# Decoder block: the negated row maxima go into the transposed queries by a copy and two DMAs instead of two broadcasts

## The reference

```python
x = layernorm(x + attn(x))        # kernelised attention, 16 heads of 16, 64 random features
x = layernorm(x + xattn(ctx, x))  # softmax attention, queries from x, keys and values from ctx
x = layernorm(x + ffn(x))         # gated, activations to 8 bits, weights ternary
```

```python
kh, qh, vh = ctx_h @ Wk.T, x_h @ Wq.T, ctx_h @ Wv.T
attn = softmax(qh @ kh.T / sqrt(16))
out_h = attn @ vh
```

## Time and profile before

| | |
|---|---|
| time, median of 3 runs | 572.56 us (571.44 to 573.2) |
| profiled execution, span | 572.7 us |
| PE busy | 498.8 us, 87% |
| DVE busy | 473.8 us, 83% |
| ACT busy | 468.6 us, 82% |
| POOL busy | 387.8 us, 68% |
| mean granted clock of PE | 0.959 |

### The profile page before, as it was taken

How to read it: one execution, slowest core, us unless ns; L and a number is a source line. 1 busy time by engine, 2 the same in 40 slices (tenths; PEclk the granted TensorE clock), 3 DMA queues, 4 the chain that set the end, 5 groups by cost and what they waited for, 6 DMA issues and landing times.

```text
span 572.7 us, 17406 instructions
## 1 busy us (share of the span) xinstructions
PE 498.8 (87%) x5990; PEld 346.3 (60%) x5990; DVE 473.8 (83%) x1380; ACT 468.6 (82%) x843; POOL 387.8 (68%) x769
## 2 busy tenths in 40 slices
PE   3057999999999999999999999999999998977751
PEld 2034777666667666677776777776766666744310
DVE  0783566888989998999999999999999998998671
ACT  0225678999999998999999999999999999987631
POOL 7032665678776777777777777787788876665432
PEclk9995999999999999999999999999999999997775
DMA  5604765656676765656565656665555677353221
GB/s 137 220 0 76 139 121 110 105 119 113 132 129 131 130 118 111 130 118 130 112 127 116 129 114 126 121 125 116 124 121 120 127 122 120 84 113 65 36 48 37
DMA packets 191625, 64.01 MB, mean 112 GB/s; under 512 B 171360, under 2 KB 191328, under 8 KB 191584
## 3 DMA queue, kind: packets, MB, share of 16 engines
q1 hardware_dynamic: 189056, 60.32, 53.5%
q10 hardware_dynamic: 2528, 3.15, 1.7%
HBM read 17.31 MB, written 4.19 MB: 38 GB/s over the span
## 4 chain that ended last, share of the span: by engine, by line
ACT 25%; POOL 21%; PE 20%; issue 11%; DVE 9%; DMA 8%; SPq 4%; ACTq 1%; POOLq 1%; DVEq 0%
DMA hqT<-hq 6%; ACT tT L610 5%; PE bank L1081 4%; POOL pkA L410 4%; POOL hq L465 4%; POOL hq L470 3%; POOL rs L424 3%; ACT pT L616 2%; PE bank L1148 2%; ACT pT L617 2%; SPq L303 2%; ACT x L549 2%; POOL y L414 2%; ACT pkA L505 2%; PE bank L1294 2%
## 5 line engine op out<-in xcount | busy, mean ns | idle before, releaser
L1081 PE MATMUL bank<-wq_hi,xT 128*128 128x512 f16 (+1 forms) x256 | 72.0, 337 | 0.3
L610 ACT ACTIVATE tT<-bank 16x1024 f16<-16x1024 f16 x64 | 65.0, 1016 | 1.2
L460 POOL TENSOR_TENSOR xq<-xm,nmagic 128x256 bf16<-128x256 f32 x32 | 19.6, 614 | 66.4 <-DVE xm L908 66.4
L1148 PEld LDWEIGHTS bank<-kvm,phq 128*128 128x128 f32 x512 | 62.2, 192 | 2.5
L1148 PE MATMUL bank<-kvm,phq 128*128 128x34 f32 x512 | 59.8, 272 | 0.0
L410 POOL TENSOR_TENSOR pkA<-qk,pkA 128x512 f16<-128x512 f32 x32 | 37.5, 1173 | 32.9 <-ACT pkA L505 32.9
L424 POOL TENSOR_TENSOR rs<-ve,mhalf 128x1 f32<-128x1 f32 x96 | 52.8, 550 | 0.0
L1294 PE MATMUL bank<-downT,hqT 128*128 128x256 bf16 x256 | 34.6, 280 | 16.5 <-DMA hqT<-hq 16.4
L862 DVE TENSOR_REDUCE negm<-bank 128x4 f16<-128x512 f32 x64 | 43.8, 684 | 5.5 <-PE bank L1197 5.1
L1241 PE MATMUL bank<-pT,ctxv 128*32 128x128 f32 x1024 | 41.6, 281 | 6.8 <-ACT pT L617 6.7
L912 DVE SCALAR_TENSOR_TENSOR g<-th,bank 128x512 f32<-128x512 f32 x64 | 43.3, 676 | 4.0 <-ACT th L640 3.8
(11 more groups left out here) (180 smaller groups left out, 1637.3 us busy)
## 6 DMA issues: line engine op xcount, KB each, us to landing
xs<-in_x_dram SPq DMA_DIRECT2D x32, 128.0 KB, 2.7
xr<-in_x_dram SPq DMA_DIRECT2D x32, 128.0 KB, 2.5
cs<-in_ctx_dram SPq DMA_DIRECT2D x32, 128.0 KB, 2.6
out_dram<-ot SPq DMA_DIRECT2D x32, 128.0 KB, 2.1
ffn_ld<-in_L_ffn_w_gate_dram ACTq DMA_DIRECT2D x1, 1024.0 KB, 5.8
ffn_ld<-in_L_ffn_w_up_dram ACTq DMA_DIRECT2D x1, 1024.0 KB, 8.7
ffn_ld<-in_L_ffn_w_down_dram ACTq DMA_DIRECT2D x1, 1024.0 KB, 10.6
pkAT<-pkA SPq DMA_TRANSPOSE x64, 3.3
```

The lines of the kernel that those rows point to most:

```text
L610: last = sc.activation(tT[p + 32:p + 48, :, :], at_mT.bitcast(F16)[p + 32:p + 48, :].unsqueeze(1).to_broadcast([DK, PAIRS, P]), ACT.Copy)
L1081: last = T.matmul(o, xT[:, 2 * part + c, :], w[:, c, cols], start=(n == 0), stop=(n == 5))
L1148: last = T.matmul(at_num[:, 2 * DV * k:2 * DV * (k + 1)], phq[:, par, k, :], kvm[:, k, :, :].rearrange("p h d -> p (h d)"), start=False, s ...
```

## The change

One copy of 128x128 takes the transposed maxima from PSUM to a new tile nmT, and SP moves 8 partitions of it into one partition of tT, twice: nmT rows 32 to 39 to partition 32, rows 96 to 103 to partition 96. The 8 rows of maxima, one per pair, thus lie one behind the other along a single partition. The one-hot of pkC becomes a 1 in the first element of slot 2, and the other 15 rows of the slot, zero on both sides, stay zero from the transposed pkT. tT gets two buffers, `tT_` and `cT_` wait for `st1` of two tiles before, and `st0` waits for the two DMAs instead of `mT`.

```diff
-        tT = sb("tT", [P, PAIRS, P], F16)
+        tT = sb("tT", [P, 2, PAIRS, P], F16)
+        nmT = sb("nmT", [P, P], F16)
...
-                wait_ahead(sp, t, ("clo", 0))
+                wait_ahead(sp, t, ("clo", 0), ("st1", -2))
...
-                wait_ahead(sp, t, ("tlo", 0), ("st1", -1))
-                transpose(tT[:, :, :], pkT[:, :, :, :].rearrange("p h r d -> p (h r d)"), "tT", par)
+                wait_ahead(sp, t, ("tlo", 0), ("st1", -2))
+                transpose(tT[:, par, :, :], pkT[:, :, :, :].rearrange("p h r d -> p (h r d)"), "tT", par)
+
+            def row(t, par):
+
+                wait(sp, "mT", t)
+                for p in (32, 96):
+                    sp.dma_start(tT[p:p + 1, par, :, :], nmT[p:p + PAIRS, :]).then_inc(moved["row"][par], 16)
...
                 go(qT, i, par, 2)
+                go(row, i, par, 6)
                 go(tT_, i, par, 5)
...
-            for par in range(2):
-                hot = pkC[:, par:H:2, 2, :]
-                g.affine_select(out=hot, in_=hot, compare_op=ALU.not_equal, fill=1.0, base=0,
-                                pattern=[[1, PAIRS], [-1, DK]], channel_multiplier=0).then_inc(masks, 1)
+            g.memset(pkC[:, :, 2, 0:1], 1.0).then_inc(masks, 1)
...
                 wait(act, "mTp", t)
-                for p in (0, 64):
-                    last = sc.activation(tT[p + 32:p + 48, :, :],
-                                         at_mT.bitcast(F16)[p + 32:p + 48, :].unsqueeze(1).to_broadcast(
-                                             [DK, PAIRS, P]), ACT.Copy)
-                last.then_inc(done["mT"], 1)
+                wait_moved(act, "row", t, par, -1)
+                copy(nmT[:, :], at_mT.bitcast(F16), "mT")
...
             def st0(t, par):
 
-                wait(pe, "mT", t)
+                wait_moved(pe, "row", t, par)
```

More of the change, by code:

```diff
@@ L222, in decoder_kernel @@
         ).split()}
-        moved = {name: [sem(f"s_{name}{i}") for i in range(2)] for name in ("qT", "kT", "cT", "tT", "hqT")}
+        moved = {name: [sem(f"s_{name}{i}") for i in range(2)] for name in ("qT", "kT", "cT", "tT", "hqT", "row")}
         def wait_moved(eng, name, t, par, off=0):
             if not isinstance(t, int) or t + off >= 0:
-                eng.wait_ge(moved[name][(par + off) % 2], (t + off - (par + off) % 2) * 8 + 16)
+                each = 32 if name == "row" else 16
+                eng.wait_ge(moved[name][(par + off) % 2], (t + off - (par + off) % 2) * (each // 2) + each)
         def wait(eng, name, t, off=0):
@@ L374, in _ @@
                             pattern=[[0, PAIRS], [-64, 2], [0, DV]], channel_multiplier=1).then_inc(masks, 1)
-            for par in range(2):
-                hot = pkC[:, par:H:2, 2, :]
-                g.affine_select(out=hot, in_=hot, compare_op=ALU.not_equal, fill=1.0, base=0,
-                                pattern=[[1, PAIRS], [-1, DK]], channel_multiplier=0).then_inc(masks, 1)
-            pool.wait_ge(masks, 6)
+            g.memset(pkC[:, :, 2, 0:1], 1.0).then_inc(masks, 1)
+            pool.wait_ge(masks, 5)
             g.affine_select(out=mask8[:, :], in_=mask8[:, :], compare_op=ALU.is_ge, fill=0.0, base=DK - 1,
@@ L384, in _ @@
                             pattern=[[0, PAIRS], [64, 2], [0, DV]], channel_multiplier=-1).then_inc(masks, 1)
-            pool.wait_ge(masks, 8)
+            pool.wait_ge(masks, 7)
             pool.wait_ge(b_in, 64)
@@ L690, in _ @@
             v.tensor_copy(xwv_rep[:, :, :], xw_ld[:, 2, :].unsqueeze(1).to_broadcast([DK, 8, DK])).then_inc(rep, 1)
-            dve.wait_ge(masks, 8)
+            dve.wait_ge(masks, 7)
             v.tensor_reduce(mask2[:, :], mask8[:, :].rearrange("p (s h) -> p h s", h=2), AX, ALU.add).then_inc(prep, 1)
@@ L1035, in _ @@
             pe.wait_ge(rep, 6)
-            pe.wait_ge(masks, 8)
+            pe.wait_ge(masks, 7)
             def ffn_means():
@@ L1195, in s0 @@
                 for k in range(4):
-                    T.matmul(at_s0a[:, k * P:(k + 1) * P], tT[0:64, k, :], cT[0:64, par, k, :], start=True, stop=True)
-                    last = T.matmul(at_s0b[:, k * P:(k + 1) * P], tT[64:128, k, :], cT[64:128, par, k, :],
+                    T.matmul(at_s0a[:, k * P:(k + 1) * P], tT[0:64, par, k, :], cT[0:64, par, k, :], start=True, stop=True)
+                    last = T.matmul(at_s0b[:, k * P:(k + 1) * P], tT[64:128, par, k, :], cT[64:128, par, k, :],
                                     start=True, stop=True)
@@ L1204, in s1 @@
                 for k in range(4):
-                    T.matmul(at_s1a[:, k * P:(k + 1) * P], tT[0:64, 4 + k, :], cT[0:64, par, 4 + k, :],
+                    T.matmul(at_s1a[:, k * P:(k + 1) * P], tT[0:64, par, 4 + k, :], cT[0:64, par, 4 + k, :],
                              start=True, stop=True)
-                    last = T.matmul(at_s1b[:, k * P:(k + 1) * P], tT[64:128, 4 + k, :], cT[64:128, par, 4 + k, :],
+                    last = T.matmul(at_s1b[:, k * P:(k + 1) * P], tT[64:128, par, 4 + k, :], cT[64:128, par, 4 + k, :],
                                     start=True, stop=True)
@@ L1216, in st0 @@
             def st0(t, par):
-                wait(pe, "mT", t)
+                wait_moved(pe, "row", t, par)
                 wait(pe, "hu1", t, -2)
                 for k in range(4):
-                    T.matmul(at_st0a[:, k * P:(k + 1) * P], cT[0:64, par, k, :], tT[0:64, k, :], start=True, stop=True)
-                    last = T.matmul(at_st0b[:, k * P:(k + 1) * P], cT[64:128, par, k, :], tT[64:128, k, :],
+                    T.matmul(at_st0a[:, k * P:(k + 1) * P], cT[0:64, par, k, :], tT[0:64, par, k, :], start=True, stop=True)
+                    last = T.matmul(at_st0b[:, k * P:(k + 1) * P], cT[64:128, par, k, :], tT[64:128, par, k, :],
                                     start=True, stop=True)
@@ L1228, in st1 @@
                 for k in range(4):
-                    T.matmul(at_st1a[:, k * P:(k + 1) * P], cT[0:64, par, 4 + k, :], tT[0:64, 4 + k, :],
+                    T.matmul(at_st1a[:, k * P:(k + 1) * P], cT[0:64, par, 4 + k, :], tT[0:64, par, 4 + k, :],
                              start=True, stop=True)
-                    last = T.matmul(at_st1b[:, k * P:(k + 1) * P], cT[64:128, par, 4 + k, :], tT[64:128, 4 + k, :],
+                    last = T.matmul(at_st1b[:, k * P:(k + 1) * P], cT[64:128, par, 4 + k, :], tT[64:128, par, 4 + k, :],
                                     start=True, stop=True)
```

## The result

The changed kernel takes 566.41 us (median of 4 runs, 565.91 to 568.16), the kernel before 572.07 beside it. The ratio is 0.9896, with a 95% interval of 0.9866 to 0.9925: 5.7 us faster, about half of the 11.2 that were forecast. The same kernel, measured again in experiment 12, had a ratio of 0.9901. The profiled execution of the changed kernel spans 564.2 us and took 565.91.

What follows compares the result with a forecast made beforehand. ACT was taken as the bound at a 14.83 us period, PE 2% behind. Middle 4.2, before it 5.0, ramp 0 and tail 2.0 made 11.2: 572.7 - 11.2 = 561.5 us, range 556 to 573.

Steps and rivals of the forecast that it cites:

- rival A: Middle loop: PE bounds and the row DMAs are hidden; 561.5 us, between 556 and 566; chance 0.62.
- B: At st0: row partly exposed, landing at 2.2 to 2.4 us stalls 0.1 to 0.3; 564 to 570 us; chance 0.17.
- The bound of before: Middle loop: ACT's queue with the two broadcasts of mT sets the 14.83 us period; PE is 2% behind.
- The saving on ACT: ACT's queue: two activations, 2.04 us, replaced by a copy of 0.26, about 0.2 in the queue; 1.84 us saved per iteration.
- The middle, 4.2 us: Middle loop: 14 periods each give back 0.3 us, PE's slack, down to a floor of 14.53 us.
- The stretch to tile 17, 5.0 us: Before the middle, 100 to 240 us: five PE waits at dn shorten by some 3.8 us, small waits add 1.2.
- The ramp, 0: Ramp, at st0: new path 2.5 us against 2.0, a loss of 0.5 once or twice, given back at tT_; 0.
- The margin of 0.4 us: At st0 in the middle: the row may take 2.1 us before PE stalls, and lands in 1.6 to 1.7.
- The tail, 2.0: Tail: six more iterations with mT on the chain gain 0.3 to 0.4 us each, 2.0 us in all.
- The second buffer, 0: tT's second buffer: removes the tT_ wait for st1; tT arrives up to 1 us earlier at an unwaiting s0; worth 0.
- C: Row path becomes the loop, from a landing of 2.4 us; 578 us at 2.6, 589 at 3.0; chance 0.10.
- D: Another loop, through DVE, needs 14.8 us, so nothing comes back; 571 to 573 us; chance 0.11.

Runs made afterwards that it cites:

- experiment 12: The changed kernel again, unaltered, beside the kernel before: 567.21 us, ratio 0.9901.
- experiment 4: The changed kernel with two activations of the old size put back on ACT behind the copy: 578.63 us, ratio 1.0082.
- experiment 6: The kernel before, with the product of the low part of x left out of the v projection on PE: ratio 1.0, period 14.80.
- the second profile: Another profile of the changed kernel, nothing altered: span 566.0 us, against 564.2 in the profile shown first.
- experiment 1: The kernel before with only the second buffer of tT and the st1 waits moved two tiles back: 572.94 us, ratio 0.998.
- experiment 3: The changed kernel without the two row DMAs, st0 waiting only for the copy, maxima not subtracted: 565.69 us, ratio 0.985.
- experiment 10: The changed kernel with all 16 rows of maxima moved by a single DMA instead of two: 564.92 us, ratio 0.9868.
- experiment 9: The changed kernel with a third row DMA, to partition 33, which meets only zeros: 581.9 us, ratio 1.016.

## Why the prediction was right, and where it was off

The direction and the mechanism came out: ACT's queue stopped being the bound, PE took over, and the row was hidden in the middle. The size did not: 5.7 us against 11.2. The measured 566.41 lies within the stated 556 to 573, but 0.4 above rival A's own 556 to 566 and inside B's 564 to 570, though the landing, 1.67 us, was on A's side of its mark of 2.1. That the range held owes as much to its width as to the sum.

**The bound of before.** Right. ACT's queue with the two broadcasts set 14.83: experiment 4 puts it back, experiment 6 shows that PE work then costs nothing.

**The saving on ACT.** Right. The copy took 0.30 us against 0.26, and ACT's load fell by 57.4 / 32 = 1.79 us per tile against 1.84. The saving of 1.87 that the prediction adds by the figures of the Trainium skill ("ScalarE: Activation LUTs", the section on what ACT_TABLE_LOAD costs) is not quite what they give: an estimated 1.88 with the overlap taken off the copy alone, and 1.69 with it taken off all three. The measured 1.79 lies between.

**The middle, 4.2 us.** Right within its size: 207.6 - 204.0 = 3.6. The floor of PE was taken as 14.53, and it is 14.57. That a loop of PE with DVE's `ad3` lies 0.04 us under PE's own queue, and the row's path 0.2 us, was not in the prediction.

**The stretch to tile 17, 5.0 us.** Mis-sized. It measured 3.5 in the pair of profiles, 2.9 with the second profile, and 2.1 to 2.7 against the 137.1 of experiments 1 and 6. PE's idle time for hqT went from 4.8 us to

```profile
PE bank L1297 <- DMA hqT<-hq: 2.5, 4, 1.4
```

and to 3.0 in the second profile, where the sum had 1.0 left. The step took the five waits for lateness of ACT. Three of them, 4.0 of the 4.8 us, follow landings of hqT that took 4.7 to 4.9 us instead of 3.3, as the chain of the kernel before shows (start us, us, what):

```profile
133.72 4.89 DMA hqT<-hq
...
164.62 4.85 DMA hqT<-hq
...
210.95 4.71 DMA hqT<-hq
...
227.50 3.27 DMA hqT<-hq
```

A shorter queue on ACT issues hqT earlier but doesn't shorten a landing: the wait of 1.4 us left in the changed kernel follows one of 4.81. And part of the 3.5 is luck: the landing issued at 133.3 took 3.43 in that profile and 4.82 in the second. What goes with the long landings stands in the last section.

**The ramp, 0.** This step failed too. I wrote a loss of 0.5 once or twice, given back at `tT_`. It is 1.6 us from tile 3 to 8, three times some 0.5. How much of it is still there at tile 17 is open: from tile 3 to 17 the changed kernel takes 190.1 and 190.7, the one without row DMAs 188.5, but the one with one DMA 190.1. In the ramp `st0` has nothing to hide behind; the chain of the changed kernel at tile 7:

```profile
93.93 0.28 ACT nmT L511
...
94.23 0.67 SPq L331
...
94.96 1.67 DMA tT<-nmT
```

0.28 + 0.73 + 1.67 and the gaps between make 2.7 us, against 2.1 for the two broadcasts at the same tile of the kernel before. Of the terms of the path the landing was right (1.67, predicted 1.6 to 1.7) and the issue was wrong: 0.73 us each, where I took 0.47 from the spacing of the 128 KB transfers. I had taken 8 runs of 256 bytes to issue no slower than 128 rows of 1 KB. The margin of 0.4 us in the middle so shrank to 0.2. Experiments 3 and 10 show the price in the ramp: with one DMA or none it takes 53.8 and 53.7, against 54.1 before.

**The tail, 2.0.** 1.8 and 1.3 against the profile of the kernel before. Against the 115.2 of experiment 1 it is 0.8 and 0.3, so its size is not settled; the clock changes level several times there.

**The second buffer, 0.** Wrong in the kernel it belongs to. Alone it is worth about 1 us, with the shorter ACT it is worth 3. The step said that tT arrives at an `s0` that doesn't wait for it, which is true, and stopped there. It didn't ask what is queued behind `tT_` on SP: hqT, seven issues and 7.1 us later, for which PE does wait. The total was not touched, because the gain of 0.3 per iteration contained it: a right number for a step whose reason was incomplete.

**The sum.** The pair of profiles as it stands gives 1.2 - 1.6 + 3.5 + 3.6 + 1.8 = 8.5, which is more than the times differ by. Against the profile of experiment 1, whose kernel is about 1 us faster than the one before, it is 0.1 - 1.6 + 2.7 + 3.5 + 0.8 = 5.5. The terms of single profiles are good to some 0.7 us each outside the middle, so that this comes near 5.7 proves no single one. Besides, the prediction was made against a profile 0.9 to 2.6 us longer than the median spans of the kernel before, and its 561.5 is a span, which the times exceed by 1.7 at the least.

**The rivals.** C's turning point was put at a landing of 2.4 us and its price at 1 us per us above it; experiment 9 went there by the issue instead of the landing and found the turning point at 0.2 us of extra path, and a price of 0.54 for 0.7. A has happened in the middle. In the ramp the row is exposed as in B, but by its issue and not by a landing of 2.2 to 2.4. D's loop exists, at 14.53 and not 14.8. The fixed part of about 2.0 us per DMA that the Trainium skill gives ("DMA: Bandwidth & Descriptors", the section with the two cost components) compares with 1.67 here from the start of the issue to the landing, for 2 KB from SBUF to SBUF; the Trainium skill fits its figure on DMAs that GpSimd issues. Here the measured 1.67 decides: the row landed sooner than by that figure.

## What to carry to other kernels

When one queue has been relieved, read the queues that ran beside it again: here SP's run of seven issues and a loop through DVE stood 0.1 to 0.3 us under the old bound, and a buffer worth about 1 us before was worth half of the gain after. A small DMA in place of an engine's copy is a trade of throughput for latency: here it cost nothing in the middle, where 3.6 us of other work stand between, and 0.5 us per tile in the ramp, where its 2.7 us stand on the path. Join small transfers first: here every issue added 0.7 us to the path. Before a wait goes into a sum, look whether the transfer behind it took its usual time. And look at the granted clock of a stretch before reading an edit into its length.

## What the runs showed of the hardware

A direct DMA of 8 runs of 256 bytes from SBUF to SBUF held SP's queue for 0.66 us in the median (0.63 to 0.81 in the changed kernel's profile), longer than one of 128 rows of 1 KB to or from HBM (medians 0.34 to 0.42, single ones up to 1.55).

hqT lands in 3.3 us as a rule, and in nearly 5 now and then, in the written-out iterations and in the first turn of the hardware loop (start us, us, what):

```profile
471.17 4.96 DMA hqT<-hq
```

Among the packets of that stretch one of 16,384 bytes on the instruction queue starts between 474.0 and 474.5 and takes 0.88 us, and the mean time of the 256-byte packets there is 112 ns instead of 21. The page of the profile counts 24 packets on that queue, 0.39 MB in all:

```profile
q8 instruction: 24, 0.39, 0.3%
```

The other traces bear this out. In the 14 profiles 66 landings of hqT took 4.2 us or more, and in each of them a packet of 16,384 bytes on the instruction queue was under way between issue and landing. All 66 are in the written-out iterations or the first turn of the loop. Between 250 and 445 us, in the later turns, no such packet appears, and 190 landings took 3.05 to 3.46 us. Of the 156 other landings without such a packet the longest took 4.18. The reverse doesn't hold: with 36 such packets the landing stayed under 4.2, mostly when the packet began in the first 1.1 us or close to the end. So loads of instructions go together with landings 0.9 to 2.0 us longer. That was read, not tested: no run changed how the instructions are loaded.
